# State-space scans in a hybrid kernel: the two products of C with its decays on VectorE in place of GpSimd

## What is computed

```python
def step(state, inp):
    dA_t, dt_t, B_t, C_t, x_t = inp
    state = state * dA_t[:, :, None, None] + (dt_t[:, :, None] * x_t)[..., None] * B_t[:, None, None, :]
    y = jnp.einsum('bhpn,bn->bhp', state, C_t)
    return (state, y)
```

## Time and profile before

| what | value |
|---|---|
| median of 3 runs | 1012.92 us (1011.82 to 1015.36) |
| profiled execution: span, first to last instruction | 1012.5 us |
| profiled execution: its own time | not listed apart from the three runs; the median lies 0.4 us above the span |
| mean granted clock of TensorE, as a share of full | 0.938 |
| share of the span busy: PE, DVE, ACT, POOL | 87%, 73%, 52%, 25% |
| one batch of the scans (from one `g_sb` L1750 to the next, 473.46 to 530.19 us) | 56.7 us |

### The profile page before, as it was taken

How to read it: one execution, slowest core, us unless ns; L and a number is a source line. 1 busy time by engine, 2 the same in 40 slices (tenths; PEclk the granted TensorE clock), 3 DMA queues, 4 the chain that set the end, 5 groups by cost and what they waited for, 6 DMA issues and landing times.

```text
span 1012.5 us, 19616 instructions
## 1 busy us (share of the span) xinstructions
PE 879.7 (87%) x7534; PEld 686.5 (68%) x7534; DVE 740.6 (73%) x1959; ACT 522.8 (52%) x796; POOL 250.1 (25%) x250
## 2 busy tenths in 40 slices
PE   3788999999988797979787979798779899989997
PEld 2556565656575675867566767676568788878887
DVE  2867677767766768696859595856968877878785
ACT  1525445544577465646464646453334665456543
POOL 0035111011100534343325252527520111011100
PEclk9879999999999697989799989899999999999999
DMA  5531000000003030302030303031000000000000
GB/s 146 177 134 22 11 11 21 22 11 12 21 1 67 7 73 5 70 20 54 10 64 2 73 2 73 2 73 64 2 1 1 22 22 22 1 22 22 22 3 40
DMA packets 30892, 36.13 MB, mean 36 GB/s; under 512 B 4560, under 2 KB 24912, under 8 KB 30800
## 3 DMA queue, kind: packets, MB, share of 16 engines
q1 hardware_dynamic: 29648, 30.68, 12.4%
q10 hardware_dynamic: 1152, 4.19, 1.1%
HBM read 21.50 MB, written 4.98 MB: 26 GB/s over the span
## 4 chain that ended last, share of the span: by engine, by line
PE 60%; DVE 25%; ACT 6%; issue 5%; POOL 2%; SPq 0%; DMA 0%; DVEq 0%; ACTq 0%; POOLq 0%
PE ps L1028 7%; PE ps L699 6%; DVE cacc L1693 4%; PE ps L950 4%; PE ps L686 4%; PE ps L778 3%; DVE acc L1970 3%; PE ps L780 3%; PE ps L779 3%; PE ps L653 3%; PE ps L941 2%; PE ps L658 2%; ACT un L1359 2%; PE ps L934 2%; PE ps L675 2%
## 5 line engine op out<-in xcount | busy, mean ns | idle before, releaser
L1970 DVE SCALAR_TENSOR_TENSOR acc<-ps,comb,acc 128x128 f32<-128x128 f32 x512 | 141.2, 344 | 22.2 <-PE ps L1028 21.7
L1028 PEld LDWEIGHTS ps<-w_f,hid 128*128 128x128 f32 x1024 | 131.2, 191 | 16.2 <-ACT hid L1378 8.0
L1378 ACT ACTIVATE hid<-ps,b_f 128x512 f32<-128x512 f32 x128 | 86.1, 685 | 107.5 <-PE ps L780 107.4
L1028 PE MATMUL ps<-w_f,hid 128*128 128x128 f32 x1024 | 136.8, 276 | 4.6 <-ACT hid L1378 4.6
L569 POOL TENSOR_TENSOR srs<-sve,neg_half 128x1 f32<-128x1 f32 x64 | 50.8, 794 | 217.3 <-DVE gram L1802 217.3
L1550 DVE TENSOR_REDUCE nmax<-ps 128x1 f32<-128x1024 f32 x64 | 78.1, 1221 | 30.7 <-PE ps L658 30.4
L1693 DVE SCALAR_TENSOR_TENSOR cacc<-ps,cw,cacc 128x1023 f32<-128x1023 f32 (+5 forms) x72 | 91.8, 1275 | 10.4 <-ACT cacc L1250 9.6
L1319 ACT ACTIVATE dcy<-ps 128x1024 f32<-128x1024 f32 x64 | 65.0, 1016 | 59.0 <-PE ps L901 58.9
L1166 ACT ACTIVATE probs<-ps,nmax 128x1024 f32<-128x1024 f32 x64 | 71.2, 1113 | 38.7 <-DVE nmax L1550 35.8
L1785 DVE SCALAR_TENSOR_TENSOR dcy<-dcy,g_sb 128x1024 f32<-128x1024 f32 x64 | 86.1, 1346 | 0.1
L686 PEld LDWEIGHTS ps<-id_f,probs 128*128 128x128 f32 x512 | 59.9, 144 | 33.1 <-issue 23.5
(11 more groups left out here) (212 smaller groups left out, 1905.0 us busy)
## 6 DMA issues: line engine op xcount, KB each, us to landing
c_dec<-exp_dram SPq DMA_DIRECT2D x32, 256.0 KB, 5.2
xc<-in_x SPq DMA_DIRECT2D x8, 512.0 KB, 3.6
q_b<-q_a SPq DMA_DIRECT2D x16, 256.0 KB, 2.8
X<-in_x_tok ACTq DMA_DIRECT2D x8, 512.0 KB, 5.5
c_rep<-cacc SPq DMA_DIRECT2D x32, 128.0 KB, 3.1
out<-o_ch SPq DMA_DIRECT2D x8, 512.0 KB, 2.6
w_f<-in_w SPq DMA_DIRECT2D x2, 512.0 KB, 4.2
cst_f<-in_sel_rows SPq DMA_DIRECT2D x1, 512.0 KB, 4.5
```

What stands on the lines that cost most here:

```text
L1028: last = nc.tensor.matmul(ps[:, Y_BANKS[n], t * P:(t + 1) * P], hid[n % 2][:, t * P:(t + 1) * P], w2_f[:, e, :], start=True, stop=True)
L1378: nc.scalar.activation(hid[n % 2][:], ps[:, 4 + n % 2, :], ACT.Gelu, bias=b1_f[:, n // 2:n // 2 + 1]).then_inc(e_hidden_ready, 1)
L1970: done = nc.vector.scalar_tensor_tensor(acc[u][:, tt, :], ps[:, bank, t * P:(t + 1) * P], comb[u][:, tt, e:e + 1], acc[u][:, tt, :], ALU.m ...
```

## The change

The two products are taken from POOL's table and from its list ahead of the scans, and put into DVE's, with the same two waits (for `decf` and for `c_rep`; on DVE only ahead of the first of the two). In the tables POOL had them at slots 3.5 and 4.5; DVE has them at 4.5 and 5.5, first among the pieces of those slots, so behind `mean_square` of chunks 4 and 5 and ahead of a tap. For batch 0 they stand on DVE behind `mixed(0)` and ahead of `softplus`. Shapes, types and buffers stay.

```diff
-            def decayed(b, u, g):
-
-                pool.wait_ge(m_decf_ready, 2 * b + 2)
-                pool.wait_ge(m_c_spread, 64 * (b + 1))
-                rows = c_dec[u][:, 1:NT, g, :]
-                nc.gpsimd.tensor_tensor(rows, rows, c_rep[:, P:N].rearrange("p (c t) -> p c t", t=P),
-                                        ALU.mult).then_inc(m_c_decayed, 1)
-
...
-            pool_parts = [(totals, (), 3.5), (decayed, (0,), 3.5), (decayed, (1,), 4.5), (weighted, (0,), 5.5),
+            pool_parts = [(totals, (), 3.5),   (weighted, (0,), 5.5),
                           (weighted, (1,), 6.5)]
...
             totals(0, 0)
-            decayed(0, 0, 0)
-            decayed(0, 0, 1)
             operand(0, 0, 0)
...
+                def decayed(g):
+
+                    if g == 0:
+                        dve.wait_ge(m_decf_ready, 2 * b + 2)
+                        dve.wait_ge(m_c_spread, 64 * (b + 1))
+                    rows = c_dec[u][:, 1:NT, g, :]
+                    nc.vector.tensor_tensor(rows, rows, c_rep[:, P:N].rearrange("p (c t) -> p c t", t=P),
+                                            ALU.mult).then_inc(m_c_decayed, 1)
...
-            dve_parts = [("conv", (2, 3), 1, -0.25), ("ends", (), 1, 1), ("low", (), 2, 2.75), ("inner", (), 1, 3),
+            dve_parts = [("decayed", (0,), 1, 4.5), ("decayed", (1,), 1, 5.5), ("conv", (2, 3), 1, -0.25), ("ends", (), 1, 1), ("low", (), 2, 2.75), ("inner", (), 1, 3),
...
             mixed(0)
+            for g in range(2):
+                fronts[0]["decayed"](g)
             fronts[1]["softplus"](0)
```

More of the change, by code:

```diff
@@ L1753, in inner @@
                     dve.wait_ge(m_inner_ready, b + 1)
-                return {"low": low, "steps": steps, "conv": conv, "softplus": softplus, "exponents": exponents,
+                def decayed(g):
[5 more added lines that the diff above has]
+                                            ALU.mult).then_inc(m_c_decayed, 1)
+                return {"decayed": decayed, "low": low, "steps": steps, "conv": conv, "softplus": softplus, "exponents": exponents,
                         "ends": ends, "inner": inner}
             fronts = [front(b, b % 2) for b in range(B)]
-            dve_parts = [("conv", (2, 3), 1, -0.25), ("ends", (), 1, 1), ("low", (), 2, 2.75), ("inner", (), 1, 3),
+            dve_parts = [("decayed", (0,), 1, 4.5), ("decayed", (1,), 1, 5.5), ("conv", (2, 3), 1, -0.25), ("ends", (), 1, 1), ("low", (), 2, 2.75), ("inner", (), 1, 3),
                          ("steps", (), 2, 4), ("conv", (0, 1), 2, 4), ("conv", (0, 2), 2, 4.5),
```

## The result

The changed kernel takes **1020.5 us** (median of 12 runs, 1016.8 to 1024.4) against 1012.4 us of the kernel before (12 runs, 1007.1 to 1020.3): ratio 1.0073, 95% interval 1.0049 to 1.0098, so 5 to 10 us slower. The forecast was 1024 us, 11 us slower, with a range of 1018 to 1031.

What follows compares the result with a forecast made beforehand. DVE alone was taken to bound from `y_w` of chunk 4 to `cumulate`. Six batches at 1.6 us (9.6), 1.7 ahead of the scans and -0.3 in batch 6 sum to 11.0; on 1012.9 that is 1024 us, range 1018 to 1031.

Steps and rivals of the forecast that it cites:

- What bounds: From `y_w` of chunk 4 to `cumulate`, 14.8 us of a batch, DVE alone sets the time; work put there is added.
- The product: One product on DVE: 1.07 us long, 0.99 of the engine's time, taken as 1.0; sixteen make 16 us.
- 0.28 back: Batches 0 to 5, in the bound stretch: L1785 and L1715 lose stalls from POOL, 0.28 us a batch.
- 0.12 back: Batches 0 to 5: L1720, held by POOL's `weighted`, gains 0.12 us because `weighted` starts some 0.15 us earlier against DVE's tap.
- worth 0: Batches 0 to 5: L1708 loses 1.4 us of stall, off the path ahead of DVE's waits for ACT and PE: 0.
- Ahead of the scans: Both products between `mixed(0)` and L1715 cost 2.0 us, less 0.3 of L1721's stall: 1.7 us.
- Batch 6: POOL's product no longer holds `mixed`, `xdt` and root; at most 1.2 us back over two chunks, taken as -0.3 us.
- 0.4 (wait for the root behind an undisturbed `mixed`): Batch 6: DVE would still wait 0.4 us for POOL's root, part of 3.4 us of DVE's time per chunk.
- PE is next to bound: Batch 6: with this and the root between product and `mixed`, the gain was taken as 0.3 us, from at most 1.2.
- The first, the clock: Rival, chance 0.15: longer PE idle ahead of `cumulate` means more half-clock work, 6 to 12 us more, about 1033.
- The second rival, products hidden: Rival, chance 0.07: DVE's 2.68 us idle ahead of `y_w` of chunk 7 takes up the products; 1013 to 1016 us.
- The third, faster by the port: Rival, chance 0.04: every stall given back, L1708's included, lies on the path, products fall into DVE's idle; 11.8 us faster, 1001.

Runs made afterwards that it cites:

- e3: Changed kernel with DVE's products moved to slot 2 and, ahead of the scans, behind the inner products; POOL's `totals` at slot 0.5: 1005.6 us, ratio 0.9957 to before.
- e9: Changed kernel with both products on DVE at slot 3.5 and POOL's `totals` at slot 0.5: 1009.3 us, ratio 0.9962 to the kernel before.
- e10: Changed kernel with POOL's two `weighted` products moved to slots 2.5 and 3.5, the C products left on DVE: 1019.6 us, ratio 1.0073 to the kernel before.
- e1: Changed kernel without the products on any engine, DVE only raising the semaphore: 1007.4 us, ratio 0.9963 to the kernel before.
- e2: Kernel before with only batch 7's two products, made during batch 6, on DVE: 1010.7 us, ratio 1.0002 to the kernel before.
- e5: Changed kernel with one more 128x768 product on DVE ahead of each product of batches 1 to 6: 1033.6 us, ratio 1.0212 to the kernel before.
- e8: e3 with POOL's two `weighted` products also moved, to slots 2.5 and 3.5: 995.1 us, ratio 0.9826 to the kernel before.
- e6: Changed kernel with the first head group's product on POOL at slot 3.5, the second on DVE at 5.5: 1011.6 us, ratio 0.9991 to the kernel before.

## Why the prediction was right, and where it was off

**What bounds.** Right. DVE alone sets the time from `y_w` of chunk 4 to `cumulate`; e3 and e9 show it, by 12 and 11 us (from the ratios) between places on the same engine. One sign was off: PE's wait ahead of `cumulate` was to grow by 0.5 to 1 us each, and PE to wait a second time for `y_w` of chunk 5. The wait grew by about 1.5, and PE's waits show no second one.

**The product.** 1.07 us long and 0.99 of the engine's time by the neighbour's rows; measured 1.09 and 1.00 (e10: 2.01 for two). The formula of the Trainium skill ("VectorE: DVE Perf Modes", section "The TRN2 errata") gave 1.09, and the rows now show 1.086 on average.

**The stalls given back in the stretch.** "0.28 back" and "0.12 back" came out as 0.30 (14.77 to 14.47, e1) and 0.22 (L1710, 1.36 to 1.14): 0.52 for 0.4, so net 1.49 us per batch for the forecast's 1.6. L1708's 1.4 us were "worth 0", as forecast: its gain, 1.6 us, went into DVE's waits, in a chunk in which PE is busy from end to end.

**Ahead of the scans.** 1.7 us forecast. From the start of `mixed(0)` to `y_w` of chunk 0 the two traces have 8.43 us (341.46 to 349.89) and 10.13 us (343.18 to 353.31): 1.70. To `y_w` of chunk 1, the place that the forecast named, it is 2.04 (18.52 and 20.56).

**Batch 6 was mis-sized.** "At most 1.2 comes back ... I take -0.3 us" was -1.95 (12.04 to 10.09; e2 shows it alone). The mechanism, POOL's product in front of `mixed`, `xdt` and root, was right. In the two chunks with products 8.10 us fell to 6.29, so 1.8 came back and not 1.2; the third gave 0.14. The first error is "0.4 (wait for the root behind an undisturbed `mixed`)", which does not occur: the root gets its input between product and `mixed` and then runs beside `mixed`, without holding it. DVE's own instructions then take 3.0 us a chunk, not 3.4. The second is the discount from 1.2 to 0.3 because "PE is next to bound". PE does bound, but only just above that: its products follow each other without a gap, and a chunk takes 3.15 us. With no products at all (e1) a chunk takes the same 3.15 us, with DVE waiting 0.58 us for PE. First two rows of PE in the changed kernel, in the chunk that begins at 695.90, then DVE in e1:

```profile
698.34 0.65 PE L931 MATMUL ps<-dcy,xdt 128*32 128x128 f32 x16
698.91 0.73 PE L891 MATMUL ps<-rhs_c,lhs_c 128*128 128x512 f32 x2
```

```profile
689.69 0.42 DVE L1842 TENSOR_TENSOR y_w<-ps,zs 128x256 f32<-128x256 f32 x1 [0.58 <-PE ps L931]
```

So DVE's two products cost nothing in these chunks either.

**Sum.** Path terms as measured: 1.70 ahead of the scans, 1.53 in batch 0 (chunks 4 to 7, 21.07 to 22.60), 5 x 1.49, -1.95 in batch 6, together 8.7 us. The forecast's 11.0 was over by 2.3, of which 1.65 are batch 6. Measured are 8.1 us by the medians, 5 to 10 by the interval. That 8.7 and 8.1 lie so close is partly luck, since the two spans differ by 5.4 us only. Beside the path's 8.7 the changed kernel's execution had 1.7 us more ahead of `mixed(0)`, and less in places that the change doesn't touch: 1.0 in the chunks 0 to 3, 2.4 in the tails, 1.7 in batch 7's chunks 4 to 7.

**The rivals.** The first, the clock, did not come: the stretch and not the clock carries the loss, and the tails got shorter. But the argument against it was wrong too. "One that is a us longer moves the restart and with it the rise, and lengthens no work" doesn't hold: before, in batch 2, the clock was still at half in the window from 502, 3.6 us and more behind the restart at 498.45, and rose at about 505.2 (the window from 504 has 0.71); in the changed kernel the restart is at 504.81 and the clock is up again from about 509.5 (windows of 2 us, the granted clock third from the right):

```profile
500.00:502.00 2.00, 0.00 (x0) 0.00 (x0) 2.00 (x4) 0.69 (x1) 0.00 (x0) 1.00 0.00 0
502.00:504.00 2.00, 0.00 (x0) 0.00 (x0) 1.97 (x5) 0.00 (x0) 0.45 (x1) 0.66 0.00 0
504.00:506.00 2.00, 1.19 (x5) 1.10 (x6) 2.00 (x2) 0.00 (x0) 1.54 (x2) 0.50 0.00 0
...
508.00:510.00 2.00, 2.00 (x26) 1.51 (x28) 0.85 (x1) 0.11 (x1) 0.00 (x0) 0.63 0.14 33
```

6.7 us of work at half clock there, 4.7 here. The fall and the rise are not tied to stop and restart by a fixed time. This tail is the shorter one (5.89 for 6.72 us); in e10 and e5 the tails are longer. For the change itself its part can't be told from the scatter of one program (e2). The second rival, products hidden, fell: the stretch grew by 1.49 us, and the wait ahead of `y_w` of chunk 7 did not take it up. The third, faster by the port, fell where it was said to: DVE's gain at L1708 went into the wait for ACT.

**What stays open** is why the time of e10 is 6 us over what its path gives, and why its clock is the lower one. The tails, chunk 3 of a batch and batch 7 hold the us in the profiles, and the granted clock falls there, but no run fixed the clock's falls, so this is argued, not shown. PE's stop in batch 3 is not explained either.

## What to carry to other kernels

Here an instruction moved to an engine twice as fast cost its full 1.0 us, less the stalls it took away, because it entered a stretch in which the new engine is last; look for the stretch, not at the shares. Before changing the engine try the slot: here the same products cost 11 us at slots 4.5 and 5.5 of DVE and nothing at slot 2, and on the slower engine, early enough, they cost nothing either. A small instruction that takes many times its length in one place (L1708, 2.13 for 0.22 us; L1720, 1.36) pointed here to an instruction of the other engine that reads the same memory. L1720 stands in the stretch that bounds, and moving that neighbour gave 10 to 13 us (e8 against e3, by medians and by ratios); L1708 stands outside it, and freeing it gave nothing. And before a difference of a few us between two profiles is explained, look for jumps like those of chunk 3 and of batch 3.

## What the runs showed of the hardware

- A POOL instruction need not hold DVE to its own end. In batch 6 of the changed kernel DVE's L1784, with two inputs in SBUF, started at 697.45 and took its undisturbed 1.22 us, though POOL's root ran until 697.94 (the two fences on batch 6 above). The Trainium skill, "SBUF — State Buffer", section "Who interferes with whom", has the pair held for the whole instruction; this agrees with POOL's products (L1708 ended with them), not with the root, a power of one element per partition. A longer power shows it as well: in the kernel before POOL's L517 (128 x 16) ran from 340.38 to 343.27, and DVE's L1785 started beside it at 341.46 and took 1.22 us.
- The granted clock fell 1.7 us behind PE's stop in one execution (batch 2 of before: PE's last product ended at 493.26, the clock fell at about 494.9, with 0.73 in the window 494 to 496) and 4.5 us behind it in another (changed: 498.16 and about 502.6), with PE doing the same products ahead of the stop.
- Two executions with the same instructions in batches 1 to 5 (before and e2) differ by about 1 us in the tail of one batch (6.58 and 5.70 us in batch 3, 6.71 and 5.69 in batch 4).
- The clock also falls while PE has no gap: the same 73 products, PE busy throughout, took 7.02, 8.54 and 10.15 us at a mean granted clock of 1.00, 0.80 and 0.66 (batches 4 and 5 of before, batch 3 of e2).
- PE can stand still for 4.64 us in the middle of a run of products with no wait that the profile shows (changed, at 521.07), and not do so in another execution (e6, where the chunk takes 5.94 for 13.28 us). In the changed kernel the granted clock was 0.50 in the three windows of 2 us from 520 to 526.
